# Layer norm's normalised input computed on GpSimd instead of VectorE, in an attention kernel of two layers

## The reference, cut to what matters

```python
def _layernorm(x, w, b, eps=1e-05):
    mu = jnp.mean(x, axis=-1, keepdims=True)
    xc = x - mu
    var = jnp.mean(xc * xc, axis=-1, keepdims=True)
    return xc * jax.lax.rsqrt(var + eps) * w + b

# first layer, 8 heads of 32 channels
x = _layernorm(x1d, norm_w, norm_b)          # x1d = group norm of the input
qkv = (x @ qkv_w.T)
gate = jax.nn.sigmoid(x @ gate_w.T + gate_b)
weights = jax.nn.softmax(q k^T + bias, over keys)
out = (weights @ v) * gate @ final_w.T + final_b
```

## Time and profile before

| | us |
|---|---|
| median of 3 runs | 3881.66 |
| lowest, highest of the 3 | 3876.53, 3882.25 |
| time of the profiled execution | 3882.37 |
| span of the profiled execution | 3880.5 |
| PE (TensorE matmul) busy | 3584.0 |
| DVE (VectorE) busy | 3097.5 |
| ACT (ScalarE) busy | 2583.5 |
| POOL (GpSimd) busy | 1994.2 |

### The profile page before, as it was taken

How to read it: one execution, slowest core, us unless ns; L and a number is a source line. 1 busy time by engine, 2 the same in 40 slices (tenths; PEclk the granted TensorE clock), 3 DMA queues, 4 the chain that set the end, 5 groups by cost and what they waited for, 6 DMA issues and landing times.

```text
span 3880.5 us, 120998 instructions
## 1 busy us (share of the span) xinstructions
PE 3584.0 (92%) x36234; PEld 3025.6 (78%) x36234; DVE 3097.5 (80%) x11357; ACT 2583.5 (67%) x8615; POOL 1994.2 (51%) x3722
## 2 busy tenths in 40 slices
PE   4579999999999999999999997999999999999998
PEld 1167778778877787878877876888888888888887
DVE  4479999999999999999999996666667676666666
ACT  1158888888888888888888884555555555555554
POOL 0056666666666666666766663333333333333333
PEclk7589999999999999999999998999999999999999
DMA  9911111111111111111111110111111111111111
GB/s 366 350 44 50 48 42 49 49 49 42 47 49 49 46 43 49 49 49 41 49 49 49 45 44 31 44 43 49 43 49 43 49 43 49 43 49 45 47 47 41
DMA packets 189031, 238.40 MB, mean 61 GB/s; under 512 B 11824, under 2 KB 176176, under 8 KB 184752
## 3 DMA queue, kind: packets, MB, share of 16 engines
q1 hardware_dynamic: 184368, 204.17, 16.6%
q10 hardware_dynamic: 4608, 33.56, 2.3%
HBM read 170.57 MB, written 67.11 MB: 61 GB/s over the span
## 4 chain that ended last, share of the span: by engine, by line
PE 48%; DVE 18%; issue 13%; POOL 10%; ACT 5%; DMA 3%; DVEq 1%; ACTq 0%; POOLq 0%; SPq 0%
PE work L453 22%; PE work L462 5%; POOL prob L354 5%; PE turn L493 5%; PE turn L601 5%; PE mix L614 5%; ACT prob L686 4%; PE score L480 3%; DMA x_chunk<-xT 3%; PE score L584 3%; DVE att L999 2%; DVE kT L920 2%; POOL g_tok L368 2%; POOL g_tok L365 2%; DVE att L905 2%
## 5 line engine op out<-in xcount | busy, mean ns | idle before, releaser
L354 POOL TENSOR_SCALAR prob<-prob,row_inv 128x256 f32<-128x256 f32 x2048 | 1049.2, 530 | 681.0 <-DVE row_inv L874 668.4
L453 PE MATMUL work<-src,w 128*128 128x256 f32 x7680 | 1075.8, 289 | 40.1 <-DVE y_sb L856 29.9
L453 PEld LDWEIGHTS work<-src,w 128*128 128x128 f32 x7680 | 946.6, 189 | 161.8 <-issue 84.5
L686 ACT ACTIVATE prob<-prob,row_min 128x256 f32<-128x256 f32 x2048 | 1022.9, 504 | 38.9 <-DVE row_min L868 38.9
L868 DVE CUSTOM_DVE_ANT_0 prob<-score,neg_bias 128x256 f32<-128x256 f32 x2048 | 752.9, 419 | 112.2 <-PE score L480 101.5
L406 POOL TENSOR_SCALAR prob<-prob,row_inv 128x160 f32<-128x160 f32 x1024 | 387.8, 397 | 668.6 <-DVE row_inv L992 668.6
L748 ACT ACTIVATE prob<-prob,row_min 128x160 f32<-128x160 f32 x1024 | 426.5, 418 | 437.8 <-DVE row_min L971 437.8
L493 PE MATMUL turn<-ident,prob 128*128 128x128 f32 x4096 | 626.3, 275 | 35.4 <-DVE probT L879 29.9
L692 ACT COPY probT<-turn 128x512 f32<-128x512 f32 x512 | 299.4, 585 | 349.5 <-PE turn L493 349.5
L493 PEld LDWEIGHTS turn<-ident,prob 128*128 128x128 f32 x4096 | 462.7, 141 | 78.5 <-POOL prob L354 47.8
L453 PE MATMUL work<-att,wf 128*128 128x256 f32 x3072 | 433.4, 291 | 19.1 <-DVE att L999 2.3
(11 more groups left out here) (86 smaller groups left out, 5316.1 us busy)
## 6 DMA issues: line engine op xcount, KB each, us to landing
pair_chunk<-pairT ACTq DMA_DIRECT2D x32, 1024.0 KB, 7.5
x_chunk<-xT SPq DMA_DIRECT2D x32, 1024.0 KB, 8.0
x_sb<-xT SPq DMA_DIRECT2D x128, 256.0 KB, 3.4
x_tok<-x_nat SPq DMA_DIRECT2D x128, 256.0 KB, 3.4
x1T<-y_sb SPq DMA_DIRECT2D x128, 256.0 KB, 2.2
x_sb<-x1T SPq DMA_DIRECT2D x128, 256.0 KB, 2.9
outT<-y_sb SPq DMA_DIRECT2D x128, 256.0 KB, 2.2
prob<-w_d SPq DMA_DIRECT2D x1, 1024.0 KB, 8.4
```

Source lines behind the costliest of these rows:

```text
L354: pool.tensor_scalar(prob[:, h, ib], prob[:, h, ib], row_inv[:, h, ib:ib + 1], 1.0, ALU.mult, ALU.mult).then_inc(norm_done[0], 1)
L453: ins = pe.matmul(out[:, cb], w[:, of_w, kb, cols + cb * P:cols + (cb + 1) * P], x[:, of_x, kb], start=n == 0, stop=n == len(terms) - 1)
L686: act.activation(prob[:, h, ib], prob[:, h, ib], ACT.Exp, bias=row_min[:, h, ib:ib + 1], scale=-1.0, accum_out=row_sum[:, h, ib:ib + 1]).t ...
```

## The change

GpSimd computes `xn` itself, directly behind its power and ahead of `norms(m, 3)`. It waits for its own `ln_rstd_done`, and for `t2_done` (the transposes of the row before have read `xn`). VectorE no longer waits for `ln_rstd_done` and `t2_done`, nor does it run L932. The operation, its operands and the count of semaphore increments are the same.

```diff
@@ GpSimd, body0
                     wait(pool, ln_var_done, far.times(1, 1))
                     apart(pool, pool_passed)
                     pool.tensor_tensor(ln_rstd[:], ln_var[:], minus_half[:], ALU.pow).then_inc(ln_rstd_done, 1)
+                    wait(pool, ln_rstd_done, far.times(1, 1))
+                    wait(pool, t2_done, far.times(1, 0))
+                    apart(pool, pool_passed)
+                    for tb in range(TB):
+                        pool.tensor_scalar(xn[:, tb], g_tok[:, far.base % 2, tb], ln_mv[:, tb, 0:1],
+                                           ln_rstd[:, tb:tb + 1], ALU.subtract, ALU.mult).then_inc(xn_done, 1)
                 if m.exists:
                     norms(m, 3)
@@ VectorE, body0
                 if nxt.exists:
                     mins(nxt, 0)
                     mins(nxt, 1)
-                if far.exists:
-                    wait(dve, ln_rstd_done, far.times(1, 1))
-                    wait(dve, t2_done, far.times(1, 0))
-                    for tb in range(TB):
-                        dve.tensor_scalar(xn[:, tb], g_tok[:, far.base % 2, tb], ln_mv[:, tb, 0:1],
-                                          ln_rstd[:, tb:tb + 1], ALU.subtract, ALU.mult).then_inc(xn_done, 1)
                 if m.exists:
                     turn_copy(5)
```

## The result

The changed kernel takes 3891.98 us (median of 20 runs, 3882.80 to 3897.93). The kernel before, run beside it, takes 3883.81 us (20 runs, 3876.53 to 3890.52). The ratio is 1.0019 [1.0011, 1.0026], some 7 us. Run again later, the same kernel gave 1.0008 [1.0000, 1.0017]; weighted by their runs, the two ratios make 1.0015, 5.8 us. The forecast was 3 us the other way: 3878.4, with a range up to 3885. Of its distance to the measured time 2.2 us are its base, since the three runs that it started from have a median of 3881.66 and the 20 here 3883.81; the range would not hold the time with that added either.

A forecast was written before the change was run, and what follows sets the result against it. A chain passing between TensorE and VectorE bounds each row, with `turns(5)` releasing the copy, not `xn`. Steady rows 0, added cost 0, edges 3.25 us off 3882.37 give 3879.1, less 0.7 is 3878.4 us; range 3872 to 3885.

The forecast's parts named there:

- The steady rows: 124 of the 128 rows: `xn` lies in the shadow of TensorE's work, so credit 0 and cost 0.
- GpSimd's price: Two `xn` instructions on GpSimd, each priced at L395's 549 ns, 1.10 us a row.
- self-wait: GpSimd's wait on its own power before `xn`: taken as 0.1 us, within bounds of 0 and 0.20.
- the 2.5 us of cover: The first two `norms(m, 3)` instructions would end 2.5 us before `turns(6)` needs them, so GpSimd's added work costs 0.
- The edges: Rows 0, 1, 2 and the last, where `xn` is on the chain: gains summing to 3.25 us.
- rows 0 to 2: First layer's first three rows: gains of 1.5, 0.8 and 0.3 us.
- the gain of 1.5: Row 0: `xn` on GpSimd comes before L365 and ends at 215.6 against 217.09.
- Row 1: TensorE would be 2.1 us earlier, but VectorE's next wait for it is only 0.83; gain 0.8 us.
- the gain of 0.65: Last row: `turns(5)` over at 2344.06, `xn` from 2345.35, so VectorE is late; all but the overlap saved.
- small stalls that a changed program could bring: Whole kernel: chance 0.02 that the forecast case lands above the 0.2% bound (7.8 us); no time given.
- the rivals: VectorE's time counts fully, 3788 us (0.02); only the 0.12 us gap won, 3863 (0.06); GpSimd late, 3928 (0.04).
- The slower one: GpSimd late at `turns(6)` if its `xn` block exceeds 3.6 us; 50 us in all, 3928 us; chance 0.04.

The follow-up runs named there:

- the kernel without `xn`: Kernel before with `xn` a constant set once: VectorE's two instructions removed, nothing put on GpSimd; 3887.63 us, 1.0004 [0.9995, 1.0013].
- the three versions of the change without it that moved no tile: Changed kernel plus: two one-column VectorE instructions into `bias_rows`, 0.9997; 36 semaphore increments between layers, 0.9994; 36 on VectorE and 92 on GpSimd, 1.0004.
- the one where it moved by eight: Changed kernel with 8 idle semaphore increments added to VectorE's program between the layers; 3889.99 us (one run).

## Why the prediction was wrong

**The steady rows: right.** No cost and no gain, in 124 rows, by the timelines and by the kernel without `xn`. Also right: the copy 0.64 us behind `turns(5)`, its new wait of 0.8 us (91.8 us in 119 rows by the waits), and no new wait of TensorE for GpSimd's L354 (40.9 us in the 119 rows before, 40.3 after).

**GpSimd's price: wrong, hidden.** "The nearest row is L395, the same operation on the same shape", 549 ns. It was the same kind of instruction with other arithmetic. At 1222 ns and a self-wait of 0.24 us (0.1 forecast), `norms(m, 3)` begins 2.3 us later (2.66 less 0.38), not 0.8. `turns(6)` began at 1005.75 in the row shown, the half it needs was ready at 1004.77 (1003.85 and half of 1.85): of the 2.5 us of cover 1.0 is left. The Trainium skill, "GPSIMD Engine Reference", Key points, has elementwise work about twice as fast on VectorE; the forecast weighed that rule against L395 and took the row. The pair is 2.43 us here for 0.73 there, more than three times; with add and multiply it would be one and a half.

**The edges: wrong.** The forecast's 3.25 us rested on that price. For rows 0 to 2 it had 2.6 us; with operations at that price 2.2 were measured, with the subtraction 0.1 and 0.8. So the reading was right and a term mis-sized. Row 0 in the timelines of GpSimd and TensorE, against the earlier trace rows:

```profile
218.61 2.42 POOL L380 TENSOR_SCALAR xn<-g_tok,ln_mv,ln_rstd 128x256 f32<-128x256 f32 x2 [0.23 <-POOL ln_rstd L375]
...
221.18 1.09 PE L558 MATMUL work<-ident,xn 128*128 128x128 f32 x4 [8.60 <-POOL xn L380]
```

The pair takes 2.42 us where VectorE, held up, had 2.68, and the transposes start 12.55 us behind the first stage's end (221.18 less 208.63), for 12.61 before; with multiply and add they start 11.21 behind it, close to the gain of 1.5 forecast for this row. Row 1 gained TensorE 1.25 us of its wait (1.14 for 2.39) and gave it back at the next: GpSimd's L368 came late, timeline of VectorE.

```profile
243.54 0.75 DVE L917 BATCH_NORM_STATS2 ln_st<-g_tok 128x6 f32<-128x256 f32 x2 [0.82 <-POOL g_tok L368]
```

At the last row the gain of 0.65 was read from a VectorE that was late. It was late by the pause at 2345.00, 0.35 us ahead of its last `xn`, which the forecast took for steady behaviour; with the code moved, that pause stands elsewhere, timelines of VectorE, GpSimd and TensorE after:

```profile
2330.61 0.69 DVE L885 COPY probT<-turn 128x512 f32<-128x512 f32 x1 [1.86 <-issue]
...
2342.14 0.49 POOL L354 TENSOR_SCALAR prob<-prob,row_inv 128x256 f32<-128x256 f32 x1 [1.12 <-issue]
...
2347.78 0.98 PE L486 MATMUL score<-kT,nqT 32*128 32x256 f32 x24 [0.91 <-issue]
```

**The step that failed** is a clause: "0.02 above, for small stalls that a changed program could bring". The forecast gave no time to them, and they are the result: 3.8 us at the second layer's exit (rows 124 to 127: mean 38.77 after, 34.93 before) and 1.2 at the first's (53.51 for 52.29), together 5.1, as the profiles differ without their first stages, and the timed runs by some 5.8. (The other stretches come out even in this sum, partly by luck: each has a spread of a us or two, and the second layer's rows 0 to 4 one of nearly three.) That the 3.8 are the pause of VectorE is shown by the table: the five profiles with the pause have 38.3 to 39.0 us there, the seven without it 34.5 to 35.5, and the one where it moved by eight 36.8. The timed runs are weaker, but agree: the three versions of the change without it that moved no tile have 0.9997, 0.9994 and 1.0004, the change itself 1.0019 and 1.0008. The 1.2 us at the first exit are less sure: pauses of VectorE and GpSimd both moved there, TensorE has one of its own, and two runs of one kernel differ by 1.9 us.

None of the rivals came. The slower one asked for GpSimd to be late at `turns(6)`; its block of `xn` is 2.4 us and the point was 3.6.

**What stays open.** That the pauses are waits for code is an inference: from the packets of the instruction queue, and from a place that counts instructions. The packets fit well at the second layer's exit: the six profiles with a pause there have two packets of q14 at it, the first of them 0.3 to 1.4 us after the pause began, and the seven without have none between 3830 and 3860 us. Why the load is not ahead of the engine there is not shown. The Trainium skill, "Runtime: NRT & Kernel Launch", Instruction fetch mechanics, has each engine's code streamed in blocks while it executes, mostly hidden, and names a taken branch out of the window as what breaks that. The pauses here lie in the unrolled rows, within some 50 us behind the point where instruction packets set in again (2321 and 3834 us in the changed kernel, on q8, a second queue with instructions, whose packets are of 16384 bytes), which agrees; at 1.1 to 3.1 us they aren't "mostly hidden". Nor is it shown why the second layer's rows 0 to 4 take 43.8 us in some profiles and 46.5 in others. And a version with the cheap price, a correct one, was not tried: it needs the mean negated for it, and its 2 us of start, 0.06%, lie below what a measurement tells.

## What to carry to other kernels

Before work is moved off an engine, look whether its time is on the chain at all; the same wait in a body without that work is the best control, and it was right here. Price the moved operation by a row with the same arithmetic on the same engine: on GpSimd the instruction with a subtraction took 2.2 times the one with an addition, so a negated mean and an addition are worth trying. Where the expected effect is below 0.3%, look at the unrolled rows behind every loop's exit for idle time that no semaphore explains: a change of program length moves such pauses on and off the chain, for several us, and some tens of semaphore increments where the engine waits anyway can move them off again.

## What was not expected of the hardware

- GpSimd's `TENSOR_SCALAR` of 128x256 with two scalars from memory: 549 ns with multiply and add, 552 with add and multiply, 1222 with subtract and multiply. VectorE does the last in some 0.4 us.
- An engine can pause 1.1 to 3.1 us at a place fixed by its count of instructions. In front of one instruction it cost 3.6 us of the row, part of it by the clock that TensorE lost in a gap of 2.08 us (granted 0.63 in the window behind it); in front of another 1.7, where TensorE's gap was 1.62 us and the granted clock stayed at 1.00.
- A new tile of 8 bytes in a partition ahead of others in SBUF: the rows of the second layer, in which TensorE is busy 297 of 300 us, took 45.81 us for four instead of 45.48, 0.7%, while the first layer's rows 8 to 120 took 1878.2 instead of 1881.1. In the windows from 2700 to 3000 us, with the tile and without:

```profile
2700.00:3000.00 300.00, 297.01 (x2726) 261.15 (x2725) 205.78 (x784) 162.83 (x606) 108.13 (x262) 1.00 0.15 45
```

```profile
2700.00:3000.00 300.00, 296.86 (x2746) 261.12 (x2745) 208.65 (x796) 162.50 (x605) 108.48 (x264) 1.00 0.15 45
```

TensorE is as busy and gets through 20 matmuls fewer. Which of the tiles behind it this comes from, and why, wasn't tried, and no profile shows their addresses.
